# Batch statistics of a graph network: squares and two weight columns in place of a matrix product

## The chip, the cores and the metric

The kernel runs on 1 core of one Trainium2 chip. The time is the device time of one execution in microseconds (us). A core has five engines that run side by side and wait for each other by semaphores: TensorE (PE, with its weight loads as PEld), VectorE (DVE), ScalarE (ACT), GpSimd (POOL) and SyncE (SP).

## The reference

A node table x of 100,000 rows of 128 float32 goes through four residual blocks over one list of 50,000 edges sorted by destination: three GCN convolutions with batch normalization, two EVE convolutions, two SAGE convolutions, one GAT convolution. The change touches the first block alone:

```
for i in range(3):
    h = gcn_conv(h, src, dst, edge_weight, Ws[i], bs[i])
    h = h + x0
    if i < 2: h = relu(h)
    mean = mean(h, axis=0);  var = mean(square(h - mean), axis=0)
    h = (h - mean) * rsqrt(var + 1e-5) * gammas[i] + betas[i]
```

Mean and variance are taken over all 100,000 rows, so they are known only when a convolution has run through; the next one applies them as a scale and a shift of each feature.

## The kernel before

Rows of the node table are worked on in chunks of 1024 (128 partitions x T = 8 tiles of D = 128 features); two chunks are a node pair. There are 98 chunks, 49 pairs. Edges come in chunks of 1024, too, 49 of them, two to a step of the edge part.

`gcn_conv` (L1846) is called three times (stages m0, m1, m2). Each stage is one block in which every engine runs its own program, written by `merged_sweep` (L902): a loop over the edge pairs, and after each edge pair a loop over the node pairs that are ready, here mostly two. `run_conv` (L1812) gives the engines their parts.

GpSimd (`pool_program`, L1051) gathers source rows by indirect DMA (L1070, eight for a chunk of edges) and scatters edge results into a table of sums (L1078, eight for a chunk). It waits for the edge results that VectorE has read out (`e_out_read`, L1075). It gathers and scatters in steps of two chunks.

The edge part (`GcnEdges`, L1275): TensorE turns the gathered rows (L1119), ScalarE scales them in m1 and m2 (L1357), VectorE weighs them (L1366) and sums the runs of one destination (L1387), TensorE multiplies by the weights (L1129), VectorE scales the result (L1399).

The node part (`GcnNodes`, L1586) for node pair m:

- TensorE turns the pair's four half chunks (`turn_nodes`, L1187), multiplies the first two by the weights (`multiply_nodes`, L1205), then runs `between`, which is `add_gram` (L1621) for the pair before, and then multiplies the other two.
- ScalarE copies the turned halves to SBUF (L1222; L1220 in m0), then makes `y1` of the pair before from `acc` by a relu or a copy (L1652), then issues the two stores of `y1` (`store_before`, L1235, with the DMA at L1250).
- VectorE adds the residual to the sums (L1669), and makes `acc` of this pair from the multiplied halves, four instructions for each half (L1683).

The statistics before: `y1` has 129 columns, the last one all ones. For each of the eight tiles of a chunk TensorE multiplies the tile by itself (L1626), a 128x129 result that adds up in one PSUM bank `gram` over all chunks: its diagonal holds the sums of squares, its last column the sums. `vector_end` (L1696) multiplies the bank by the identity (L1703), reduces it (L1706) and works out scale and shift. The semaphore `finished` tells that `y1` is made; `gram_done` tells ScalarE that `y1` may be overwritten.

## Time and profile before

| | |
|---|---|
| median of 3 runs | 15559.0 us (15490.08 to 15566.16) |
| the profiled execution | 15524.1 us |
| its span in the profile | 15522.3 us |
| TensorE matmul busy | 7445.1 us, 48% |
| GpSimd busy | 7158.8 us, 46% |
| VectorE busy | 6201.3 us, 40% |
| ScalarE busy | 4643.8 us, 30% |
| matmuls of L1626 | 4800 records, 900.2 us busy |

Busy shares are averages over stages that differ. A row of a timeline gives the start in us, the time that it covers, the engine and line, the operation with out<-in, how many there are (x), and in brackets the idle time of the engine just before and what ended it. "issue" is time in which the engine waited for nothing that the profile shows; "remote" is a releaser that the profile doesn't name.

### The profile page before, as it was taken

What the parts mean: (1) busy time and instruction counts of PE and PEld (TensorE: products, weight loads), DVE (VectorE), ACT (ScalarE), POOL (GpSimd) and SP (SyncE); (2) the same over time, 40 slices, a digit from 0 to 9 for tenths busy, and PEclk for the clock granted to TensorE, in tenths of its full rate; (3) what the DMA queues carried; (4) which work ended last, traced back from release to release, by engine and by line L of the source; (5) the groups of instructions that cost most, each with busy time, mean ns of one, the idle gap of its engine ahead of it and who ended that gap; (6) DMA issues with size and microseconds to landing.
All of it is one profiled execution on the core that took longest, in us unless ns stands there. A gap on an engine that the chain in (4) does not pass through costs nothing. (4 is left out here: it accounts for less than half of the span.)

```text
span 15522.3 us, 166135 instructions
## 1 busy us (share of the span) xinstructions
PE 7445.1 (48%) x37142; PEld 5563.3 (36%) x37143; DVE 6201.3 (40%) x16108; ACT 4643.8 (30%) x8631; POOL 7158.8 (46%) x7582
## 2 busy tenths in 40 slices
PE   1024444544544448855555555533334445455554
PEld 1024444444434444333343333333333334233332
DVE  3333443334433435422223333322223333377778
ACT  1111111211111114422233333322213334266666
POOL 4644444444444440144434443345554444566663
PEclk9986776777767779877777777766667667677776
DMA  6965554666656667644454444445545555133333
GB/s 166 208 152 168 172 166 148 209 201 196 195 179 199 198 198 254 219 149 149 154 171 147 160 160 157 158 159 172 171 153 190 184 172 198 55 109 108 110 106 102
DMA packets 1864963, 2570.85 MB, mean 166 GB/s; under 512 B 255773, under 2 KB 1369141, under 8 KB 1864662
## 3 DMA queue, kind: packets, MB, share of 16 engines
q1 hardware_dynamic: 1134168, 1627.27, 32.8%
q10 hardware_dynamic: 504726, 564.87, 11.1%
q0 software_dynamic: 225792, 375.94, 8.4%
q14 instruction: 216, 1.77, 0.0%
q8 instruction: 61, 1.00, 0.0%
HBM read 1499.62 MB, written 1129.98 MB: 169 GB/s over the span
## 5 line engine op out<-in xcount | busy, mean ns | idle before, releaser
L1078 POOL DMA_INDIRECT sums_gcn<-m_result,m_idx x1176 | 1162.3, 988 | 2312.8 <-DVE m_result L1399 1953.1
L1220 ACT ACTIVATE m_nodeT<-m_n_bank 128x512 f32<-128x512 f32 x980 | 543.7, 597 | 4158.0 <-remote 2296.5
L1626 PE MATMUL m_gram<-m_y 128*128 128x129 f32 (+1 forms) x4800 | 900.2, 336 | 1752.2 <-issue 1440.3
L1683 DVE SCALAR_TENSOR_TENSOR m_acc<-m_n_bank,m_scales,m_res_b 128x128 f32<-128x128 f32 (+1 forms) x2352 | 645.4, 343 | 2566.0 <-remote 1863.1
L1078 POOL DMA_INDIRECT sums_eve<-m_result,m_idx x784 | 762.4, 972 | 1695.4 <-DVE m_result L1515 1470.5
L1187 PE MATMUL m_n_bank<-k_ident,m_in_y 128*128 128x128 f32 x5488 | 907.3, 323 | 1273.7 <-DVE m_z L1772 729.3
L1772 DVE TENSOR_TENSOR m_z<-m_n_bank,m_in_sums 128x512 f32<-128x512 f32 (+1 forms) x784 | 513.5, 687 | 2364.8 <-remote 1280.1
L1626 PEld LDWEIGHTS m_gram<-m_y 128*128 128x128 f32 (+1 forms) x4800 | 803.0, 246 | 1822.4 <-issue 1490.1
L1078 POOL DMA_INDIRECT sums_sage<-m_result,m_idx x784 | 762.4, 973 | 1378.3 <-DVE m_result L1399 1136.4
L1070 POOL DMA_INDIRECT m_rows<-node_rows_a,m_idx x1176 | 1124.5, 956 | 354.2 <-issue 338.0
L1187 PEld LDWEIGHTS m_n_bank<-k_ident,m_in_y 128*128 128x128 f32 x5488 | 763.3, 169 | 1402.6 <-DVE m_z L1772 808.4
L1222 ACT ACTIVATE m_nodeT<-m_n_bank,k_bn 128x512 f32<-128x512 f32 x392 | 285.4, 774 | 1939.1 <-PE m_n_bank L1187 1405.0
L1070 POOL DMA_INDIRECT m_rows<-node_rows_b,m_idx x784 | 749.7, 956 | 244.9 <-issue 233.6
L1205 PE MATMUL m_n_bank<-k_gcn,m_nodeT 128*128 128x128 f32 (+1 forms) x4704 | 701.9, 308 | 117.7 <-issue 89.3
L2215 POOL DMA_INDIRECT sums_gat<-g_result,g_idx x392 | 433.1, 1105 | 684.8 <-DVE g_result L2510 573.3
L1201 PE MATMUL m_n_bank<-m_in_x,k_ident 128*128 128x512 f32 (+1 forms) x784 | 473.3, 689 | 523.4 <-ACT m_nodeT L1220 344.9
L1119 PE MATMUL m_e_turn<-k_ident,m_rows 128*128 128x128 f32 x2744 | 495.9, 312 | 469.5 <-DVE m_sums L1582 219.0
L1205 PEld LDWEIGHTS m_n_bank<-k_gcn,m_nodeT 128*128 128x128 f32 (+1 forms) x4704 | 664.7, 223 | 151.4 <-issue 120.7
L1205 PE MATMUL m_n_bank<-k_self,m_nodeT 128*128 128x128 f32 x3136 | 470.0, 309 | 431.7 <-ACT m_nodeT L1220 392.4
L1205 PEld LDWEIGHTS m_n_bank<-k_self,m_nodeT 128*128 128x128 f32 x3136 | 462.4, 224 | 556.9 <-ACT m_nodeT L1220 401.7
L759 ACT ACTIVATE m_o<-m_z,m_ln_shift,m_ln_scale 128x128 f32<-128x128 f32 x1600 | 626.6, 479 | 90.3 <-DVE m_ln_shift L748 48.5
L1129 PE MATMUL m_e_out<-k_gcn,m_sums 128*128 128x128 f32 x2352 | 397.9, 322 | 512.8 <-DVE m_result L1399 400.5
(304 smaller groups left out, 17622.8 us busy)
## 6 DMA issues: line engine op xcount, KB each, us to landing
m_in_sums<-sums_gcn SPq DMA_DIRECT2D x291, 512.0 KB
m_in_y<-node_rows_a SPq DMA_DIRECT2D x291, 512.0 KB
sums_gcn<-k_gcn_b SPq DMA_DIRECT2D x194, 512.0 KB
node_rows_a<-m_y ACTq DMA_DIRECT2D x194, 512.0 KB
m_in_x<-in_x_dram SPq DMA_DIRECT2D x194, 512.0 KB
m_in_y<-node_rows_b SPq DMA_DIRECT2D x194, 512.0 KB
sums_eve<-k_eve_b SPq DMA_DIRECT2D x194, 512.0 KB
m_in_sums<-sums_eve SPq DMA_DIRECT2D x194, 512.0 KB
```

The source lines that it names most:

```text
L759: ins = act.activation(out[0:n, j, :], z[0:n, j, :], ACT.Identity, bias=self.shift[copy][0:n, at:at + 1], scale=self.scale[copy][0:n, at:a ...
L1070: pool.indirect_dma_start(self.rows[b][:, t, :], None, self.table[:, :], bass.IndirectOffsetOnAxis(self.idx[s][:, t:t + 1], 0)).then_inc(s ...
L1078: pool.indirect_dma_start(self.node_sums[:, :], bass.IndirectOffsetOnAxis(self.idx[s][:, T + t:T + t + 1], 0), self.result[b][:, t, :], No ...
L1119: mm = pe.transpose(bank[:, n * P:(n + 1) * P], self.rows[b][:, H * (i % 2) + n, 0:D], self.k["ident"][:, :])
L1187: mm = pe.transpose(self.n_bank[i][:, t * P:t * P + n], self.buf["y"][i // 2][0:n, H * (i % 2) + t, :], self.k["ident"][0:n, 0:n])
L1201: mm = pe.matmul(self.n_bank[i][0:n, :], self.k["ident"][0:n, 0:n], half.rearrange("p t f -> p (t f)"), start=True, stop=False)
L1205: mm = pe.matmul(self.n_bank[i][0:n, t * D:(t + 1) * D], self.nodeT[:, i, t * P:t * P + n], weight[:, :], start=not add, stop=not add or t ...
L1220: act.activation(out, src, ACT.Copy).then_inc(self.n_turn_read, 1)
L1626: mm = pe.matmul(self.gram[:, 0:D + 1], self.y1[b][0:rows[b], t, 0:D], self.y1[b][0:rows[b], t, :], start=False, stop=False, skip_group_ch ...
L1683: ins = dve.scalar_tensor_tensor(out=self.acc[b][0:n, tt, :], in0=ph.node_out(i, n)[:, t, :], scalar=self.scales[b][0:n, tt:tt + 1], in1=s ...
L1772: dve.tensor_tensor(self.z[b][0:n, half, :], ph.node_out(i, n), ph.buf["sums"][b][0:n, half, :], ALU.add).then_inc(ph.n_out_read, 1)
L2215: pool.indirect_dma_start(self.node_sums[:, :], bass.IndirectOffsetOnAxis(self.idx[s][:, T + t:T + t + 1], 0), self.result[b][:, t, :], No ...
```

## The change

`y1` loses its column of ones. ScalarE gets a second step for each chunk: after the stores of a pair are issued, it squares `y1` into a new buffer `ysq`. `add_gram` waits for the new semaphore `squared` in place of `finished`, and uses `picks`, two weight matrices of two columns (one column ones, the other zeros): the first puts the sum over the partitions of each column of `y1` into row 0 of the bank, the second that of `ysq` into row 1. The moving operand is half a chunk, 512 columns. `vector_end` copies the two rows, adds their four blocks of 128 to one, and has TensorE transpose the 2x128 result; the steps after that are the same with their counts moved by one.

```diff
--- before.py
+++ after.py
@@ -1598,20 +1598,23 @@
         self.res_b = [ph.sb(f"res_b{b}", [P, T, D]) for b in range(2)]
         self.acc = [ph.sb(f"acc{b}", [P, T, D]) for b in range(2)]
 
-        self.y1 = [ph.sb(f"y1{b}", [P, T, D + 1]) for b in range(2)]
+        self.y1, self.ysq = ([ph.sb(f"{n}{b}", [P, T, D]) for b in range(2)] for n in ("y1", "ysq"))
+        self.picks = ph.sb("picks", [P, 2, 2])
+        self.in_rows, self.pair_rows, self.col_rows = (ph.sb(n, [2, w]) for n, w in (("in_rows", 512), ("pair_rows", 256), ("col_rows", D)))
         self.scales = [ph.sb(f"scales{b}", [P, T]) for b in range(2)]
         self.small = ph.sb("small", [P, 8])
-        self.diag = ph.sb("diag", [P, D])
         self.gram = ph.ps("gram", [P, 512])
-        self.ones_set = ph.sem("ones_set")
+        self.ones_set, self.squared = ph.sem("ones_set"), ph.sem("squared")
         self.scales_set, self.added, self.acc_done = ph.sem("scales_set"), ph.sem("added"), ph.sem("acc_done")
         self.gram_done, self.bn_step, self.root_step = ph.sem("gram_done"), ph.sem("bn_step"), ph.sem("root_step")
         self.grants = [(ph.nodes_turned, 2)] + [(ph.used[n], 2) for n in ph.used] + [(s, 16) for s in ph.stored]
 
     def tensor_start(self, pe):
-        pe.wait_ge(self.ones_set, 2)
+        pe.wait_ge(self.ones_set, 3)
         zeros = self.ph.k["zeros"]
-        pe.matmul(self.gram[:, 0:D + 1], zeros[:, 0:P], zeros[:, 0:D + 1], start=True, stop=False, skip_group_check=True).then_inc(self.gram_done, 1)
+        for t in range(H):
+            mm = pe.matmul(self.gram[0:2, t * D:(t + 1) * D], zeros[:, 0:2], zeros[:, 0:D], start=True, stop=False, skip_group_check=True)
+        mm.then_inc(self.gram_done, 1)
 
     def tensor(self, pe, m, scattered):
         ph = self.ph
@@ -1621,17 +1624,21 @@
     def add_gram(self, pe, m, rows):
 
         for b in range(2):
-            pe.wait_ge(self.ph.finished, 2 * m + b + 1)
-            for t in range(T):
-                mm = pe.matmul(self.gram[:, 0:D + 1], self.y1[b][0:rows[b], t, 0:D], self.y1[b][0:rows[b], t, :], start=False,
-                               stop=False, skip_group_check=True)
+            pe.wait_ge(self.squared, 2 * m + b + 1)
+            for i, y in enumerate((self.y1[b], self.ysq[b])):
+                for h in range(2):
+                    mm = pe.matmul(self.gram[0:2, :], self.picks[0:rows[b], i, :],
+                                   y[0:rows[b], h * H:(h + 1) * H, :].rearrange("p t f -> p (t f)"), start=False, stop=False,
+                                   skip_group_check=True)
             mm.then_inc(self.gram_done, 1)
 
     def tensor_end(self, pe):
         last = self.ph.sh.node_chunks - 2
         self.add_gram(pe, self.ph.sh.node_pairs, (self.ph.sh.rows(last), self.ph.sh.rows(last + 1)))
+        pe.wait_ge(self.bn_step, 3)
+        pe.transpose(self.ph.n_bank[1][:, 0:2], self.col_rows[:, :], self.ph.k["ident"][0:2, 0:2]).then_inc(self.gram_done, 1)
         if self.last:
-            pe.wait_ge(self.bn_step, 12)
+            pe.wait_ge(self.bn_step, 13)
             for i in range(2):
 
                 pe.matmul(self.ph.n_bank[0][:, i * D:(i + 1) * D], self.as_rows[2][:, i, :], self.ph.k["ident"][:, :], start=True,
@@ -1649,8 +1656,12 @@
             act.wait_ge(self.acc_done, 2 * m + b + 1)
             ph.out_free(act, m, b)
             act.wait_ge(self.gram_done, 2 * m + 1)
-            act.activation(self.y1[b][0:n, :, 0:D], self.acc[b][0:n, :, :], ACT.Copy if self.last else ACT.Relu).then_inc(ph.finished, 1)
+            act.activation(self.y1[b][0:n, :, :], self.acc[b][0:n, :, :], ACT.Copy if self.last else ACT.Relu).then_inc(ph.finished, 1)
         ph.store_before(act, m, self.y1)
+        for b in range(2):
+            n = ph.sh.rows((m - 1) * 2 + b)
+            act.wait_ge(ph.finished, 2 * m + b + 1)
+            act.activation(self.ysq[b][0:n, :, :], self.y1[b][0:n, :, :], ACT.Square).then_inc(self.squared, 1)
 
     def finish_vector(self, dve, m):
         pass
@@ -1691,7 +1702,10 @@
     def vector_start(self, dve):
         for b in range(2):
             dve.memset(self.acc[b][:, :, :], 0.0).then_inc(self.acc_done, 1)
-            dve.memset(self.y1[b][:, :, D:D + 1], 1.0).then_inc(self.ones_set, 1)
+        dve.memset(self.picks[:, :, :], 0.0).then_inc(self.ones_set, 1)
+        dve.wait_ge(self.ones_set, 1)
+        for i in range(2):
+            dve.memset(self.picks[:, i, i:i + 1], 1.0).then_inc(self.ones_set, 1)
 
     def vector_end(self, dve):
 
@@ -1700,32 +1714,37 @@
         mean, sq, var, m2, root = (self.small[:, i:i + 1] for i in range(5))
         ss, step, gram = self.next_ss, self.bn_step, self.gram
         dve.wait_ge(self.gram_done, sh.node_chunks + 3)
-        dve.tensor_tensor(self.diag[:, :], gram[:, 0:D], k["ident"][:, :], ALU.mult).then_inc(step, 1)
-        dve.tensor_scalar(mean, gram[:, D:D + 1], 1.0 / sh.n, None, ALU.mult).then_inc(step, 1)
+        dve.tensor_copy(self.in_rows[:, :], gram[0:2, :]).then_inc(step, 1)
+        dve.wait_ge(step, 1)
+        dve.tensor_tensor(self.pair_rows[:, :], self.in_rows[:, 0:256], self.in_rows[:, 256:512], ALU.add).then_inc(step, 1)
         dve.wait_ge(step, 2)
-        dve.tensor_reduce(sq, self.diag[:, :], AX.X, ALU.add).then_inc(step, 1)
+        dve.tensor_tensor(self.col_rows[:, :], self.pair_rows[:, 0:D], self.pair_rows[:, D:2 * D], ALU.add).then_inc(step, 1)
+        sums = ph.n_bank[1]
+        dve.wait_ge(self.gram_done, sh.node_chunks + 4)
+        dve.tensor_scalar(mean, sums[:, 0:1], 1.0 / sh.n, None, ALU.mult).then_inc(step, 1)
+        dve.wait_ge(step, 4)
         dve.tensor_tensor(m2, mean, mean, ALU.mult).then_inc(step, 1)
-        dve.wait_ge(step, 4)
-        dve.scalar_tensor_tensor(out=var, in0=sq, scalar=1.0 / sh.n, in1=m2, op0=ALU.mult, op1=ALU.subtract).then_inc(step, 1)
         dve.wait_ge(step, 5)
+        dve.scalar_tensor_tensor(out=var, in0=sums[:, 1:2], scalar=1.0 / sh.n, in1=m2, op0=ALU.mult, op1=ALU.subtract).then_inc(step, 1)
+        dve.wait_ge(step, 6)
         dve.tensor_scalar(var, var, 0.0, BN_EPS, ALU.max, ALU.add).then_inc(step, 1)
-        dve.wait_ge(step, 6)
+        dve.wait_ge(step, 7)
         rsqrt(dve, root, var, sq, self.root_step, 0)
         dve.tensor_tensor(ss[:, 0:1], root, gamma[:, :], ALU.mult).then_inc(step, 1)
-        dve.wait_ge(step, 7)
+        dve.wait_ge(step, 8)
         dve.tensor_tensor(m2, mean, ss[:, 0:1], ALU.mult).then_inc(step, 1)
-        dve.wait_ge(step, 8)
+        dve.wait_ge(step, 9)
         dve.tensor_tensor(ss[:, 1:2], beta[:, :], m2, ALU.subtract).then_inc(step, 1)
-        dve.wait_ge(step, 9)
+        dve.wait_ge(step, 10)
         if self.last:
             for i in range(2):
                 dve.tensor_scalar(self.as_rows[2][:, i, :], k["ones"][:, :], ss[:, i:i + 1], None, ALU.mult).then_inc(step, 1)
-            dve.wait_ge(step, 11)
+            dve.wait_ge(step, 12)
             dve.sem_inc(step, 1)
-            dve.wait_ge(self.gram_done, sh.node_chunks + 5)
+            dve.wait_ge(self.gram_done, sh.node_chunks + 6)
             for i in range(2):
                 dve.tensor_copy(self.as_rows[i][:, :], ph.n_bank[0][:, i * D:(i + 1) * D]).then_inc(step, 1)
-            dve.wait_ge(step, 14)
+            dve.wait_ge(step, 15)
 
 
 class LinearNodes:
```

## Rows read from the trace of the kernel before

**Rows 1.** The page: the span.

```profile
span 15522.3 us, 166135 instructions
```

**Rows 2.** Line L1626 by itself: durations in ns (least, median, most), first and last start.

```profile
L1626 PE MATMUL m_gram<-m_y x4800: 270/276/584, 1031.1 to 5929.1; 128*128 128x129 f32 x192
```

**Rows 3.** Waits in m1, 2562 to 4250: us in total, times, longest.

```profile
POOL sums_gcn L1078 <- DVE m_result L1399: 661.5, 25, 42.7
DVE m_acc L1683 <- remote: 623.8, 40, 30.9
...
PE m_gram L1626 <- issue: 503.0, 228, 12.5
```

**Rows 4.** Timeline of POOL in m1: two bursts' ends, and a longer pause.

```profile
2842.12 1.01 POOL L1078 DMA_INDIRECT sums_gcn<-m_result,m_idx  x1 [42.68 <-DVE m_result L1399]
...
3047.11 1.01 POOL L1078 DMA_INDIRECT sums_gcn<-m_result,m_idx  x1 [27.59 <-DVE m_result L1399]
...
3087.62 0.95 POOL L1070 DMA_INDIRECT m_rows<-node_rows_a,m_idx  x1 [0.30 <-issue]
3115.94 1.01 POOL L1078 DMA_INDIRECT sums_gcn<-m_result,m_idx  x1 [27.37 <-DVE m_result L1399]
```

**Rows 5.** Timeline of TensorE in the same cycle.

```profile
3053.14 1.95 PE L1205 MATMUL m_n_bank<-k_gcn,m_nodeT 128*128 128x128 f32 x16
3061.80 4.24 PE L1626 MATMUL m_gram<-m_y 128*128 128x129 f32 x18 [6.72 <-issue]
3067.08 0.38 PE L1626 MATMUL m_gram<-m_y 128*128 128x129 f32 x1 [1.04 <-issue]
...
3093.38 3.62 PE L1205 MATMUL m_n_bank<-k_gcn,m_nodeT 128*128 128x128 f32 x16
3096.80 2.32 PE L1187 MATMUL m_n_bank<-k_ident,m_in_y 128*128 128x128 f32 x16
...
3101.63 3.84 PE L1626 MATMUL m_gram<-m_y 128*128 128x129 f32 x32 [0.72 <-ACT m_y L1652]
3105.30 1.95 PE L1205 MATMUL m_n_bank<-k_gcn,m_nodeT 128*128 128x128 f32 x16
```

**Rows 6.** Timeline of ScalarE, the same cycle and the next (3138.40).

```profile
3063.15 3.89 ACTq L1250 DMA_DIRECT2D node_rows_b<-m_y  x2
...
3100.51 2.02 ACT L1652 ACTIVATE m_y<-m_acc 128x1024 f32<-128x1024 f32 x2
3102.99 1.40 ACTq L1250 DMA_DIRECT2D node_rows_b<-m_y  x2
...
3138.40 6.57 ACTq L1250 DMA_DIRECT2D node_rows_b<-m_y  x2
```

**Rows 7.** Timeline of VectorE, the same cycle.

```profile
3093.02 1.13 DVE L1683 SCALAR_TENSOR_TENSOR m_acc<-m_n_bank,m_scales,m_res_b 128x128 f32<-128x128 f32 x4 [15.35 <-remote]
...
3106.75 2.16 DVE L1683 SCALAR_TENSOR_TENSOR m_acc<-m_n_bank,m_scales,m_res_b 128x128 f32<-128x128 f32 x8 [2.53 <-PE m_n_bank L1205]
```

**Rows 8.** Stretches: length, busy of PE, PEld, DVE, ACT, POOL, clock, DMA share, GB/s.

```profile
3057.00:3060.00 3.00, 0.00 (x0) 0.00 (x0) 0.00 (x0) 0.12 (x1) 2.28 (x3) 1.00 0.13 50
3060.00:3063.00 3.00, 1.20 (x5) 1.20 (x6) 0.00 (x0) 2.67 (x3) 2.39 (x3) 0.51 0.53 143
```

**Rows 9.** Timeline of TensorE in the second EVE convolution: 512-column matmuls.

```profile
9036.08 2.07 PE L1201 MATMUL m_n_bank<-m_in_x,k_ident 128*128 128x512 f32 x2 [19.61 <-ACT m_nodeT L1220]
...
9041.69 1.02 PE L1201 MATMUL m_n_bank<-m_in_x,k_ident 128*128 128x512 f32 x2
9042.55 1.05 PE L1205 MATMUL m_n_bank<-k_self,m_nodeT 128*128 128x128 f32 x8
```

**Rows 10.** Waits in the first SAGE convolution, 10034 to 11510.

```profile
POOL sums_sage L1078 <- DVE m_result L1399: 472.3, 26, 40.6
```

**Rows 11.** Timeline of VectorE at the end of m1.

```profile
4245.84 0.29 DVE L1703 TENSOR_TENSOR m_diag<-m_gram,k_ident 128x128 f32<-128x128 f32 x1 [4.87 <-PE m_gram L1626]
...
4249.51 0.16 DVE L1718 TENSOR_TENSOR k_bn<-k_beta,m_small 128x1 f32<-128x1 f32 x1
```

## The prediction

> **What bounds the kernel now.** I read the page first. No engine is busy for half of the span [rows 1], so this is a kernel of waits, and the page's chain of waits speaks only of the last convolution. The changed lines run in three stages, m0, m1 and m2 (the GCN convolutions). The history of the product line is the next view: 4800 matmul records of 270/276/584 ns [rows 2], 1600 for each stage. A float32 matmul stands as two records, and one node pair has 16 matmuls, so 32 records are one pass of the statistics and a stage has 50 passes. I take m1 (2562 to 4250 us) for all three.
>
> Then the waits inside m1 [rows 3]. GpSimd waited 25 times and 661.5 us for VectorE's edge results, a mean of 26.5 us. The statistics matmuls idled 503.0 us "until issue", which is no wait for a producer that the profile knows. VectorE's accumulation waited 623.8 us for something remote.
>
> The timelines tell why. GpSimd works in bursts: indirect transfers from 3047.11 to 3088.57, then a pause of 27.37 us, next burst at 3115.94 [rows 4]. Burst plus pause is 68.8 us, and some 24 of them fill the stage. The burst's length is GpSimd's own, so whatever lengthens or shortens the pause moves the stage. One cycle holds two node pairs. The first pair's pass runs during the burst and crawls: 18 records go at once from 3061.80, after them single ones more than 1 us apart (3067.08 is one), and the other half of the multiplication comes only at 3093.38, some 5 us after the last transfer [rows 5]. That is 31.6 us for a pass whose twin in the pause takes 3.67 us (3101.63 to 3105.30) [rows 5]. VectorE shows the same crawl from its side: an accumulation whose matmul had ended by 3055.1 starts at 3093.02 [rows 5, 7]. So in a burst the pass is cheap to lengthen, up to a point, and in the pause it is paid in full. The pause in which a third node pair falls is 42.68 us instead of 27.37 [rows 4]: an exposed pair costs 15.3 us and nothing hides it.
>
> The count follows. A crawling pass idles about 31.6 - 3.84 = 27.8 us here; 503.0 us of such idling make some 18 to 20 crawling passes in a stage. I take 20 crawling and 30 exposed, and of those 30 drop one, the first, which lies in the short first burst. 29 exposed, 20 crawling, per stage.
>
> **The change part by part.**
>
> *Exposed pass, start.* Before, the pass starts when the first of the two y1 activations ends. Now it needs a square, and ScalarE squares only after both y1 (3100.51 + 2.02 = 3102.53) and after the issue of both stores (3102.99 + 1.40 = 3104.39) [rows 6]. A square reads and writes the same 128x1024 values as a y1 activation, two of which took 2.02 us; I take 1.05 us, and 0.3 us for the waits and the end of the branch ahead of it. The first square is done at about 3105.8 to 3105.9, against a start at 3101.63: +4.25 us. The second is done 1 us later and is never late. Nothing else can fill this time: TensorE's second half of the multiplication stands behind the pass, VectorE's last two accumulations wait for it (2.53 us of waiting already at 3106.75 [rows 7]), and the edge part, GpSimd's results with it, stands behind VectorE.
>
> *Exposed pass, length.* 32 records of 129 columns go, 16 records of 512 columns come (eight matmuls, two records each). That is 8192 columns in place of 4128. A pair of 512-column records took 0.86 us from its start to that of the next operation (9041.69 to 9042.55) [rows 9], so 16 take 6.9 us; the old pass took 3.67 us. +3.2 us. The 128-column weight loads that vanish were hidden: 32 loads and 32 matmuls together took 0.115 us each [rows 5]. The Trainium skill (page "TensorE: Matmul & The Clock Gate", section "LDWEIGHTS (loading the stationary operand)") prices a load by its columns, about 107 ns for 128; if that stood in the open, 32 loads would be 3.4 us, the length would come out even and the sum near 15,880 us. The row above shows that it doesn't stand in the open, and the estimate isn't used.
>
> *Exposed pass, clock.* TensorE now idles from 3100.9 to 3105.9 ahead of it. After an idle start at 3055.09 the granted clock was 1.00 until 3060 and 0.51 in the next 3 us [rows 5, 8], which are the levels 2.4 and 1.2 GHz. A pair of 512-column records took 2.07 us at the lower level against 1.02 [rows 9]. The clock comes back within a few us of steady work: 16 records took 3.62 us, the next 16 took 2.32, the next 1.95 [rows 5]. I take +1.2 us; bounds 0 (clock stays) and 6.9 (low all through). Together an exposed pass costs +8.6 us, bounds +7.4 and +14.3.
>
> *Crawling pass.* TensorE puts through 32 matmuls and loads fewer, so at the end of the crawl it has the second half of the multiplication behind it, too, which before took 3.62 us from 3093.38. But VectorE's second accumulation can't start ahead of 3093.02, where TensorE's older signal arrived; three accumulations of 1.13 us follow, and end at about 3096.5 where they ended at 3098.17. Against it stand two squares and their waits on ScalarE, behind store issues that end at 3067.04 in one burst and at 3144.97 (11.6 us ahead of the burst's end) in the next [rows 6]; with some 5 us for the squares and 7 to 14 us for the matmuls the pass still ends near where it did. I take -2 us per pass; bounds -4 (the clock is up as well) and +3 (the late burst spills over).
>
> *Waits added.* ScalarE's next work behind the squares is the next pair's turned rows or the edge activation, and both wait for TensorE operations that stand behind the pass itself, so the squares' 2.1 us cost nothing more there. SyncE and GpSimd run the same instructions; the loads that VectorE's signal frees move with it.
>
> *Ends.* At the end of each stage the diagonal product and its reduction (two of 0.29 us in the chain that starts at 4245.84 and ends 3.8 us later [rows 11]) give way to one 2x512 copy, two small adds and a transpose on TensorE with a wait each way: +1.3 us a stage, bounds 0 and 4. The new starting memsets and four small zero matmuls in place of one lie at the start beside the first gathers: 0, at most 2.
>
> *Sum.* Per stage 29 x 8.6 - 20 x 2 + 1.3 = 211 us, for three stages 633 us. The profiled execution took 15524.1 us (span 15522.3), which gives 16,157; I say 16,160 us. That run lies 0.2% below the shown median of 15559.0 and inside its runs of 15490 to 15566. With the bounds that are likely together: 29 x 7.45 - 20 x 4, three times, gives 15,930; 29 x 12 + 0, three times, gives 16,570.
>
> **Rivals.**
>
> *A, the crawl is relieved further (still slower).* If the crawl is a limit on how many instructions get through, halving the pass's instructions could free the other engines too. The sage stage has two node pairs a cycle as well and no statistics, and GpSimd's pauses there are 472.3 us over 26 [rows 10], mean 18.2 us. Add a whole new exposed pass (8.6 + 4.4 of the old one with its wait, 13.0) and the pause is 31.2, 4.7 us above 26.5: 25 x 4.7 x 3 gives about 15,880. Against it: the old signal at 3093.02 doesn't depend on what is queued behind it.
>
> *B, faster.* One mechanism: in the burst the first pair is through so early that the second pair's pass gets into the burst as well. It decides at 29 x 8.6 / 20 = 12.5 us won per crawling pass; the pause would be the sage stage's 18.2, 8.3 us less than now, 25 x 8.3 x 3 = 620 us off: 14,900. For it: 503 us of crawling sit on exactly the instructions that are halved. Against it: the second pair needs VectorE's accumulations, which the crawl holds back and the change doesn't touch. The Trainium skill (page "Runtime: NRT & Kernel Launch", section "Instruction fetch mechanics") says that a jump out of the loaded window forces a fetch; were that the crawl, a shorter loop body would end it in this way. The second pass in the same loop doesn't crawl, and the crawl ends with the burst [rows 4, 5], so I give it no more than that chance. At the deciding point itself the time would be about 15,520 (no change).
>
> *C, the squares get stuck.* ScalarE crawls in the burst as well (two store issues took 6.57 us there, 1.40 in the pause [rows 6]). If the squares are seen only when the crawl ends, the matmuls follow in the open: +9 us per crawling pass, (29 x 8.6 + 20 x 9) x 3 = 1290: 16,810.
>
> **How the numbers follow.** Forecast 0.58, A 0.15, C 0.15, B 0.07, no change (relief at the deciding point) 0.05. What a measurement of this kernel can tell from no change is about 0.5%, 78 us. Faster by more: 0.07; within: 0.05; slower: 0.88. The range holds A and the forecast and nearly reaches C's value: 15,850 to 16,770.
>
> **What would show it.** In the pause, the first statistics record starts about 4.3 us later behind the y1 pair, 16 records take 7 to 9 us, and the granted clock dips ahead of them; GpSimd's pause grows from 27.4 to 33 to 35 us while the burst stays at 41 us; stages m0 to m2 grow by about 210 us each and no other stage moves. In the burst, the second half of the multiplication is done by about 3093 in the cycle's own terms. I am wrong if the pause stays at 27 us or less, if the pass starts before the store issues end, or if 512-column records of the pass don't take 0.43 us each at full clock.

## The result, and the profile after

| | before | after |
|---|---|---|
| median | 15527.15 us (5 runs, 15490.08 to 15566.16) | 16061.56 us (5 runs, 15986.65 to 16087.5) |
| profiled execution | 15524.1 us | 15992.39 us |
| ratio | | 1.0327 (95% interval 1.0303 to 1.0351) |
| m0, m1, m2, profiled (from the first clearing of `acc` to the next, m2 to the reading of the bank) | 1666, 1690, 1678 us | 1839, 1857, 1847 us |
| GpSimd's waits for edge results in m0 to m2 | 1953.1 us | 2432.7 us |

The change costs 3.3%. The ratio is worked out from all runs of the pair; the two medians alone lie 534 us apart. The profiled executions lie 468 us apart, and in them GpSimd's waits in the three changed stages grew by 479.6 us. Its waits of the same kind in the EVE, SAGE and GAT stages moved by +23, +0.5 and -55 us. Each changed stage grew by 167 to 173 us, 509 us in all, and the rest of the kernel took 41 us less. That rest is the same code in every kernel of this text. Behind m2 it took 9518 to 9682 us in the eleven profiles of the table below, whatever was done to the statistics, so a good part of the scatter between runs lies there, and the three stages show an edit more sharply than the total does.

The page of the kernel after: the span, and the DMA queue of ScalarE's stores (packets, MB, share).

```profile
span 15990.5 us, 161683 instructions
...
q10 hardware_dynamic: 242226, 564.87, 10.0%
```

The same megabytes had stood as 504726 packets at 11.1%. y1's rows are 128 wide now, so a partition's eight tiles lie in one piece. The prediction had not seen this.

The waits in m1 of the kernel after, 2730 to 4587 us (us in total, times, longest), against [rows 3]:

```profile
POOL sums_gcn L1078 <- DVE m_result L1399: 816.8, 25, 50.7
...
DVE m_acc L1694 <- remote: 557.8, 37, 33.3
...
PE m_gram L1630 <- issue: 214.9, 17, 19.7
...
PE m_gram L1630 <- ACT m_ysq L1664: 163.6, 33, 11.9
```

The same 25 waits, 155 us longer. The statistics idle for less "until issue", and for the first time they wait for ScalarE.

GpSimd's timeline, first transfers of three bursts, against [rows 4]. The full bursts keep their length (41.06 us on the mean in both kernels), the pauses of 27.4 us are now 31 to 34:

```profile
3031.82 1.00 POOL L1078 DMA_INDIRECT sums_gcn<-m_result,m_idx  x1 [50.71 <-DVE m_result L1399]
...
3104.28 1.01 POOL L1078 DMA_INDIRECT sums_gcn<-m_result,m_idx  x1 [31.90 <-DVE m_result L1399]
...
3179.23 1.01 POOL L1078 DMA_INDIRECT sums_gcn<-m_result,m_idx  x1 [33.49 <-DVE m_result L1399]
```

TensorE in those cycles, against [rows 5]. The burst ends at 3072.39:

```profile
3059.85 3.58 PE L1630 MATMUL m_gram<-m_y,m_picks 128*2 128x512 f32 x4 [17.72 <-issue]
...
3069.38 1.05 PE L1205 MATMUL m_n_bank<-k_gcn,m_nodeT 128*128 128x128 f32 x7
3071.94 0.27 PE L1205 MATMUL m_n_bank<-k_gcn,m_nodeT 128*128 128x128 f32 x1 [1.51 <-issue]
3075.44 0.37 PE L1205 MATMUL m_n_bank<-k_gcn,m_nodeT 128*128 128x128 f32 x1 [3.23 <-issue]
3076.85 1.67 PE L1205 MATMUL m_n_bank<-k_gcn,m_nodeT 128*128 128x128 f32 x7 [1.05 <-issue]
...
3087.52 1.88 PE L1630 MATMUL m_gram<-m_y,m_picks 128*2 128x512 f32 x4 [3.63 <-ACT m_ysq L1664]
...
3092.67 1.88 PE L1630 MATMUL m_gram<-m_ysq,m_picks 128*2 128x512 f32 x4
3094.48 2.05 PE L1205 MATMUL m_n_bank<-k_gcn,m_nodeT 128*128 128x128 f32 x16
...
3159.72 2.70 PE L1630 MATMUL m_gram<-m_y,m_picks 128*2 128x512 f32 x4 [3.75 <-ACT m_ysq L1664]
3162.21 2.80 PE L1630 MATMUL m_gram<-m_ysq,m_picks 128*2 128x512 f32 x4
```

Within the burst the 16 statistics records now go through in one piece (to 3069.4) and the crawl falls on the multiplication behind them. In the pause a pass waits for the square. It then takes 6.96 us (3087.52 to 3094.48), or 8.65 us when its first half runs at a lower clock, as from 3159.72. ScalarE and VectorE in the first of these pauses, against [rows 6, 7]:

```profile
3082.78 1.99 ACT L1659 ACTIVATE m_y<-m_acc 128x1024 f32<-128x1024 f32 x2
3085.23 0.99 ACTq L1250 DMA_DIRECT2D node_rows_b<-m_y  x2
3086.41 2.00 ACT L1664 ACTIVATE m_ysq<-m_y 128x1024 f32<-128x1024 f32 x2 [1.64 <-issue]
```

```profile
3070.21 1.13 DVE L1694 SCALAR_TENSOR_TENSOR m_acc<-m_n_bank,m_scales,m_res_b 128x128 f32<-128x128 f32 x4 [29.40 <-remote]
3076.95 1.12 DVE L1694 SCALAR_TENSOR_TENSOR m_acc<-m_n_bank,m_scales,m_res_b 128x128 f32<-128x128 f32 x4 [5.61 <-remote]
...
3096.03 2.16 DVE L1694 SCALAR_TENSOR_TENSOR m_acc<-m_n_bank,m_scales,m_res_b 128x128 f32<-128x128 f32 x8 [9.12 <-PE m_n_bank L1205]
```

The squares come behind both y1 and both store issues, so the pass starts 4.74 us behind the start of the first y1 (3087.52 against 3082.78), where the old pass started 1.12 us behind it. VectorE then waits 9.12 us for the multiplication behind the pass; before it waited 2.53. The accumulation at 3070.21 also shows that what was held up in a burst need not wait for its end: it starts 2.2 us ahead of the end of the burst at 3072.39, where the one at 3093.02 in the kernel before started 4.4 us behind its burst [rows 4, 7].

The granted clock (the number behind the five engines' busy times) in the first 3 us of the two passes:

```profile
3087.60:3090.60 3.00, 3.00 (x8) 0.59 (x9) 0.00 (x0) 0.82 (x1) 0.00 (x0) 1.00 1.01 401
3159.80:3162.80 3.00, 3.00 (x5) 0.43 (x5) 0.00 (x0) 0.81 (x1) 0.00 (x0) 0.64 1.01 408
```

**One cycle in four parts.** Each kernel has 54 cycles in m0 to m2 with a full burst (over 40 us) and behind it a pause that holds the pass of one node pair. The short bursts at both ends of a stage, and pauses with two passes, are not among them. A pause splits into: from the burst's last transfer to the first y1 (what the crawl left behind), from there to the pass, the pass, and from the pass to the next burst. The means are worked out from the timelines, in us. "m0 to m2" is the length of the three stages in the one profiled execution. The last column is the time, as the ratio to the kernel before on the same chip times 15,527.

| kernel | burst end to y1 | y1 to pass | pass | pass to burst | pause | m0 to m2 | time |
|---|---|---|---|---|---|---|---|
| before | 11.92 | 1.12 | 3.84 | 10.05 | 26.92 | 5,034 | 15,527 |
| after | 9.59 | 4.74 | 8.04 | 10.25 | 32.62 | 5,543 | 16,035 |
| e1, the wait alone | 11.62 | 5.20 | 6.27 | 10.22 | 33.32 | 5,516 | 16,010 |
| e2, the length alone | 9.73 | 1.36 | 7.03 | 10.14 | 28.26 | 5,153 | 15,662 |
| e3, 256 columns | 11.72 | 4.76 | 8.72 | 10.16 | 35.36 | 5,709 | 16,204 |
| e4, rows of 129 | 9.76 | 5.16 | 8.61 | 10.26 | 33.78 | 5,623 | 16,126 |
| e5, before with rows of 128 | 11.73 | 1.11 | 3.84 | 10.08 | 26.76 | 5,010 | 15,526 |
| e6, rows, then squares | 9.71 | 1.30 | 7.17 | 10.12 | 28.29 | 5,162 | 15,678 |
| e10, squares first | 9.64 | 2.99 | 7.03 | 10.25 | 29.91 | 5,318 | 15,830 |
| e7, old pass last | 11.35 | 2.32 | 3.74 | 6.56 | 23.97 | 4,843 | 15,294 |
| e12, new pass last | 10.40 | 2.76 | 7.03 | 6.67 | 26.86 | 5,039 | 15,563 |

### The profile page after: what moved, and what is told of

The parts are those of the page before. It is cut to its first block and busy times, and to the rows that moved or that the text cites. A ratio compares the mean times of both kernels' runs of the same rounds, so it can differ in the third digit from the quotient of the medians.

```text
span 15990.5 us, 161683 instructions
## 1 busy us (share of the span) xinstructions
PE 7924.2 (50%) x34763; PEld 4994.7 (31%) x34764; DVE 6196.5 (39%) x16114; ACT 4955.6 (31%) x8931; POOL 7173.9 (45%) x7582
## 5 line engine op out<-in xcount | busy, mean ns | idle before, releaser
L1078 POOL DMA_INDIRECT sums_gcn<-m_result,m_idx x1176 | 1164.1, 990 | 2792.4 <-DVE m_result L1399 2432.7
L1187 PE MATMUL m_n_bank<-k_ident,m_in_y 128*128 128x128 f32 x5488 | 986.8, 342 | 1353.9 <-DVE m_z L1791 831.0
L1187 PEld LDWEIGHTS m_n_bank<-k_ident,m_in_y 128*128 128x128 f32 x5488 | 811.2, 177 | 1539.1 <-DVE m_z L1791 908.2
L1630 PE MATMUL m_gram<-m_y,m_picks 128*2 128x512 f32 (+1 forms) x1200 | 733.7, 745 | 1111.1 <-issue 652.6
L1630 PE MATMUL m_gram<-m_ysq,m_picks 128*2 128x512 f32 (+1 forms) x1200 | 645.4, 665 | 0.0
```

The lines of the kernel that those rows point to most:

```text
L1078: pool.indirect_dma_start(self.node_sums[:, :], bass.IndirectOffsetOnAxis(self.idx[s][:, T + t:T + t + 1], 0), self.result[b][:, t, :], No ...
L1187: mm = pe.transpose(self.n_bank[i][:, t * P:t * P + n], self.buf["y"][i // 2][0:n, H * (i % 2) + t, :], self.k["ident"][0:n, 0:n])
L1630: mm = pe.matmul(self.gram[0:2, :], self.picks[0:rows[b], i, :], y[0:rows[b], h * H:(h + 1) * H, :].rearrange("p t f -> p (t f)"), start=F ...
```

## The experiments

**e1: the wait without the new matmuls.** The edit to the kernel before:

```diff
-            pe.wait_ge(self.ph.finished, 2 * m + b + 1)
+            pe.wait_ge(self.squared, 2 * m + b + 1)
...
+            act.activation(self.ysq[b][0:n, :, :], self.y1[b][0:n, :, 0:D], ACT.Square).then_inc(self.squared, 1)
```

> The kernel before with one part of the change: ScalarE also squares the rows behind both stores, and the product pass waits for the squares, which nothing reads. Theory (start of the pass costs): an exposed pass starts 3.6 us later behind y1 (4.74 in the kernel after, 1.11 in the kernel before), its length stays 3.84 or grows to about 4.7 where the clock falls first; 87 exposed passes at 3.6 to 4.5 us are 315 to 390 us, so 15,840 to 15,920. Rival (the wait runs beside another wait and only the length costs): within 60 us of the kernel before.

Measured: 16,021 us, ratio 1.0311 (1.0270 to 1.0352). That is 101 us above the expected band, on the side of the theory; the rival is out. The start was as expected for rows of 129 (5.20 us behind y1). The clock cost more: nearly the whole short pass ran at the lower level, not only its first records. One pass of e1, and the first 3 us of it:

```profile
3527.46 6.33 PE L1627 MATMUL m_gram<-m_y 128*128 128x129 f32 x32 [4.66 <-ACT m_ysq L1658]
```

```profile
3527.50:3530.50 3.00, 3.00 (x14) 3.00 (x15) 0.00 (x0) 0.86 (x1) 0.00 (x0) 0.50 1.01 333
```

The granted clock is 0.50 in these 3 us, the level of 1.2 GHz, and 0.64 in the next 3. In the 54 cycles the pass took 5.2 to 6.8 us, never the 3.84 of before. So the wait alone, with the same matmuls as before, costs nearly what the whole change costs.

**e2: the new matmuls without the wait.** The edit to the kernel after; ScalarE's squares are gone too:

```diff
-            pe.wait_ge(self.squared, 2 * m + b + 1)
-            for i, y in enumerate((self.y1[b], self.ysq[b])):
+            pe.wait_ge(self.ph.finished, 2 * m + b + 1)
+            for i, y in enumerate((self.y1[b], self.y1[b])):
```

> The kernel after without the squares: the pass waits for y1 as before and reads y1 twice with the two weight columns (the sums of squares are left out). Theory: the pass starts 1.1 us behind y1a, stays at the full clock and lasts 7.0 us, so 87 exposed passes cost 3.2 us each (+278), the 60 passes in a burst give back 3 us each (-180): 15,600 to 15,660. Rival (start and length both lie on the path, and the burst gives nothing back): 15,800. Rival (the 7 us lie beside VectorE's work): 15,350 to 15,450.

Measured: 15,675 us, ratio 1.0087 (1.0057 to 1.0118). That is 15 us above the expected band, with the interval reaching into it, and both rivals are out. The pass took 7.03 us in 53 of the 54 cycles, +3.19, and the pause began with 2.2 us less of crawl. With 0.3 us at the start of the pass and behind it a full cycle is 1.34 us longer. Over 54 cycles that is 72 us of the 119 by which m0 to m2 grew; the rest lies in the first and last cycles of the stages.

**e3 and e4: where the shorter crawl comes from.** e3 brings the 32 records back, with no other change to the columns; e4 brings the rows of 129 back, and everything that uses `y1` takes its first 128 columns:

```diff
-                for h in range(2):
-                    mm = pe.matmul(self.gram[0:2, :], self.picks[0:rows[b], i, :],
-                                   y[0:rows[b], h * H:(h + 1) * H, :].rearrange("p t f -> p (t f)"), start=False, stop=False,
+                for h in range(4):
+                    mm = pe.matmul(self.gram[0:2, h % 2 * 256:h % 2 * 256 + 256], self.picks[0:rows[b], i, :],
+                                   y[0:rows[b], h * 2:h * 2 + 2, :].rearrange("p t f -> p (t f)"), start=False, stop=False,
```

```diff
-        self.y1, self.ysq = ([ph.sb(f"{n}{b}", [P, T, D]) for b in range(2)] for n in ("y1", "ysq"))
+        self.y1, self.ysq = ([ph.sb(f"{n}{b}", [P, T, w]) for b in range(2)] for n, w in (("y1", D + 1), ("ysq", D)))
...
```

> The kernel after with 256 columns a matmul: 32 records and 32 weight loads a pass as in the kernel before, with the same columns as in the kernel after. Theory (the burst gives back time because fewer records queue in it): the 3 us for each of 60 passes in a burst are lost again, +180 us on the kernel after (16,240), while an exposed pass stays at 7.0 to 8.7 us. Rival (what comes back in the burst is due to y1's rows of 128, whose stores have half the packets): no change from the kernel after, within 40 us of 16,060.

> The kernel after with y1's rows again 129 wide, so that its stores go out in packets of 512 bytes, 504,726 of them on ScalarE's queue instead of 242,226. Theory (records in the burst): only the two store issues grow from 0.99 to 1.40 us ahead of the squares, 0.4 us for 87 passes, +35 us on the kernel after (16,095). Rival (the packets give the time back): +120 to +180 us (16,180 to 16,240).

Measured: e3 16,187 us, ratio 1.0436 (1.0393 to 1.0478), 125 us above the kernel after instead of the 180 expected, and outside its rival's band. e4 16,128 us, ratio 1.0386 (1.0347 to 1.0425), 33 us above the figure expected and 52 below its rival's band, so neither as stated. The four parts tell them apart. With 32 records the burst end to y1 is 11.72 us again, as in the kernel before; with rows of 129 it stays at 9.76. TensorE in a burst of e3:

```profile
3337.47 1.67 PE L1630 MATMUL m_gram<-m_y,m_picks 128*2 128x256 f32 x7
3339.58 0.38 PE L1630 MATMUL m_gram<-m_y,m_picks 128*2 128x256 f32 x1 [0.43 <-issue]
...
3359.18 0.59 PE L1630 MATMUL m_gram<-m_ysq,m_picks 128*2 128x256 f32 x1 [2.21 <-issue]
3361.28 0.37 PE L1205 MATMUL m_n_bank<-k_gcn,m_nodeT 128*128 128x128 f32 x1 [1.52 <-issue]
3361.99 3.56 PE L1205 MATMUL m_n_bank<-k_gcn,m_nodeT 128*128 128x128 f32 x15 [0.34 <-issue]
```

The last records of the pass drip again, that is, they go one by one with up to 2.4 us between them, and the multiplication runs after them. How far TensorE gets can be counted in the bursts' timelines. From the start of the pass in a burst to the first idle time over 0.4 us went (records of the multiplication behind it included) 17 to 21 records in most bursts of the kernel before (129 columns, median 19, in 4.3 us), 21 to 25 in e3 (256 columns, median 23, in 6.9 us) and 22 to 25 in the kernel after (512 columns, median 24, in 10.3 us). The time differs by a factor of 2.4 between the first and the last and the columns by 4, the count by a quarter; and e1, with the matmuls of the kernel before, has 20 to 24. What is given back in the burst comes from the number of records. It is 2.1 to 2.3 us a cycle. The rest of e3's longer pause is its pass, 8.72 against 8.04 us: 5 of its 54 passes took 7.1 us, the length at full clock, where 23 of the kernel after took 7.0.

e4 costs 0.42 us more at the start (its two store issues are 1.40 us long) and 0.57 us more of lowered clock in the pass: +1.16 us a pause, 63 us over 54 cycles, of the 80 us that m0 to m2 are longer. In e4 46 of the 54 passes took 8.7 us, in the kernel after 29: the later start is what the expectation priced, the clock behind it is what it left out. So rows of 128 do help the new kernel, by a shorter issue that stands ahead of the squares.

**e5: rows of 128 in the kernel before.** The column of ones, and with it the means, is left out.

> The kernel before with y1 in rows of 128, without the column of ones (the sums of y1, so the means, are left out): its stores go out in packets of 4,096 bytes, nothing else changes. Theory: in the kernel before the pass does not stand behind the store issues, so the 0.4 us of shorter issue and the smaller number of packets bring 0 to 30 us: 15,500 to 15,540. Rival (the packets hold up what runs in a burst): 15,400 or less.

Measured: 15,518 us, ratio 0.9999 (0.9975 to 1.0023). That is inside the expected band; the rival is out. Half as many packets on the queue bring nothing where no one waits for the issue.

**e6: rows first, then squares.** The edit to the kernel after (the matmuls below it then read `y[b]`, and `gram_done` is counted up in the second round alone):

```diff
-        for b in range(2):
-            pe.wait_ge(self.squared, 2 * m + b + 1)
-            for i, y in enumerate((self.y1[b], self.ysq[b])):
+        for i, (ready, y) in enumerate(((self.ph.finished, self.y1), (self.squared, self.ysq))):
+            for b in range(2):
+                pe.wait_ge(ready, 2 * m + b + 1)
```

> The whole statistics of the kernel after in another order: TensorE first sums the rows of both halves, on y1 alone, then the squares of both. Theory: the first 8 records (3.5 us) fill the time in which ScalarE issues the stores and squares, so the pass starts 1.1 us behind y1a, the clock stays at 1.00, and it ends about 8.3 us behind y1a, as in the run without squares: 15,660 to 15,720. Rival (ScalarE's squares themselves hold up the node work behind them): 15,800 or more.

Measured: 15,688 us, ratio 1.0097 (1.0061 to 1.0133), as expected and as e2, where no squares are made. Half of the pass now fills the wait for the squares:

```profile
3990.84 3.60 PE L1630 MATMUL m_gram<-m_y,m_picks 128*2 128x512 f32 x8
3994.48 3.59 PE L1630 MATMUL m_gram<-m_ysq,m_picks 128*2 128x512 f32 x8
```

The same statistics in another order take back 2.3 of the 3.3%.

**e10: the squares ahead of the stores.** In `finish_scalar` the loop with the squares is put before `store_before`.

> The kernel after with the squares ahead of both store issues. Theory: the pass starts 3.7 us behind y1a instead of 4.74, TensorE idles 2.6 us ahead of it, so that the clock stays at 1.00 and the pass at 7.03 us in every cycle (mean 8.2 in the kernel after): 2.2 us for 87 passes, 190 us less than the kernel after, 15,850 to 15,900. Rival (the stores, 2 us later, hold up the next y1 or the burst): 15,980 to 16,060.

Measured: 15,853 us, ratio 1.0195 (1.0154 to 1.0237), as expected in size. The start was better than I had it (2.99 us behind the first y1, not 3.7) and the clock stayed up, as expected: 7.03 us for the pass in each of the 54. The later stores cost nothing that shows: the parts ahead of y1 and behind the pass are 9.64 and 10.25 us, against 9.59 and 10.25.

```profile
3999.38 1.88 PE L1630 MATMUL m_gram<-m_y,m_picks 128*2 128x512 f32 x4 [2.01 <-ACT m_ysq L1663]
```

**e7: the old pass behind the last multiplication.** The edit to the kernel before, in `multiply_nodes`:

```diff
         for i in range(4):
-            if i == 2 and between:
-                between()
...
             mm.then_inc(self.n_multiplied, 1)
+        if between:
+            between()
```

> The kernel before with the product pass behind the last multiplication of a node pair instead of between the second and the third. Theory (the exposed pass costs because VectorE's additions of the third and fourth multiplication wait for it): these start 3.8 us earlier in 87 exposed cycles, while the pass runs beside them: 15,200 to 15,350. Rival (the edge matmuls behind the node work then wait for the same pass): within 50 us of the kernel before.

Measured: 15,302 us, ratio 0.9850 (0.9814 to 0.9886): inside the expected band, faster than both kernels and the fastest on this kind of chip. TensorE and VectorE in one pause of e7:

```profile
3078.37 3.74 PE L1203 MATMUL m_n_bank<-k_gcn,m_nodeT 128*128 128x128 f32 x32
3081.95 3.74 PE L1626 MATMUL m_gram<-m_y 128*128 128x129 f32 x32
3085.52 0.60 PE L1119 MATMUL m_e_turn<-k_ident,m_rows 128*128 128x128 f32 x4
```

```profile
3081.10 2.16 DVE L1683 SCALAR_TENSOR_TENSOR m_acc<-m_n_bank,m_scales,m_res_b 128x128 f32<-128x128 f32 x8 [0.60 <-ACT m_y L1652]
3083.84 2.16 DVE L1683 SCALAR_TENSOR_TENSOR m_acc<-m_n_bank,m_scales,m_res_b 128x128 f32<-128x128 f32 x8 [0.58 <-DVE m_acc L1683]
```

All four multiplications are done before the pass, and VectorE's two accumulations (3081.10 to 3086.00) run beside it. The pass ends at 3085.5, when VectorE would not have been free anyway. Most of the 3.84 us is hidden: 2.95 us of pause are gone, 2.39 of them behind y1 and 0.57 ahead of it.

**e8, e9, e11: three kernels on a chip that runs them faster.** e8 is e6 with the pass last, e11 is the kernel after with the pass last, e9 is the kernel before with one product a half chunk in place of eight.

> Rows then squares (as in the run with rows first), and the pass behind the last multiplication of the pair. Theory: the third and fourth multiplication no longer wait for 8.3 us of pass; VectorE's additions cover about 4 us of it, as with the product pass, where 2.7 us an exposed pass came back: 235 to 350 us less than with rows first (15,690), so 15,340 to 15,460. Rival (the longer pass now holds up the edge matmuls behind it): no gain, 15,640 to 15,700.

> The kernel before with one product a half instead of eight, 4 records a pass instead of 32 (the statistics are left out but for one tile in eight). Theory: an exposed pass costs 3.4 us less (87 times, 295 us), and in a burst 28 fewer records at the 0.13 us a record that the run with 256 columns showed (125 us over 60 passes and 16 records) give 3.6 us in 60 passes (220 us): 15,000 to 15,080. Rival (records in the burst are free, only the exposed length counts): 15,230 to 15,260.

> The kernel after with nothing changed but the place of the pass: behind the last multiplication. Theory: VectorE's additions no longer wait for squares and pass (12 us behind y1a), but the edge matmuls behind it do; the pass ends as late as before less the 2 us of the multiplications that now fill the wait, so 87 exposed passes give back 4 to 5 us each: 15,620 to 15,720. Rival (the wait for squares goes on holding TensorE for as long, and the edges for as much): 15,950 to 16,060.

Measured, on one chip: the kernel before 10,917 us (19 runs, 10,893.59 to 10,929.37), e8 10,924 (ratio 1.0010, 1.0000 to 1.0019), e9 10,901 (0.9984, 0.9974 to 0.9993), e11 11,153 (1.0224, 1.0207 to 1.0241). The kernel before is the very program that takes 15,530 us elsewhere, so none of the three tests its expectation. They show something else. GpSimd's waits and the busy row (PE, PEld, DVE, ACT, POOL, clock, DMA share, GB/s) of e8 in 2000 to 2900 us, within m1:

```profile
POOL sums_gcn L1078 <- issue: 102.4, 336, 0.3
POOL m_rows L1070 <- issue: 101.0, 352, 0.3
```

```profile
2000.00:2900.00 900.00, 741.83 (x3862) 455.98 (x3863) 573.51 (x1685) 364.88 (x439) 693.67 (x742) 0.93 0.90 325
```

There is no pause: 760 transfers follow each other from 1964.4 to 2944.1, and TensorE's passes go through in one piece beside them (8 records in 3.60 us). Nothing crawls, and GpSimd's own issue sets the stage. The statistics cost next to nothing there, long or short: e9 without most of them gains 0.2%, e8 with the long ones loses 0.1%. Of the three only e11, where TensorE also stands still for the squares, makes GpSimd wait again. GpSimd's waits of e11 in the same stretch (the wait of this name is 0.3 us in e9 and does not appear in e8):

```profile
POOL sums_gcn L1078 <- DVE m_result L1399: 59.3, 17, 9.1
```

**e12: e8 once more, on a chip of the first kind.**

> The kernel of the run e8 again, for a chip on which the kernel before takes 15,540 us and TensorE's records drip in GpSimd's bursts. Theory there: VectorE's additions cover about 4 us of the 7.2 us pass, as with the product pass, where 2.7 us an exposed pass came back: 235 to 350 us less than with rows first (15,690), so 15,340 to 15,460. Rival (the longer pass then holds up the edge matmuls by all it no longer holds up the additions): 15,640 to 15,700. On a chip where the kernel before takes 10,920 us: 10,920 as in e8, within 30 us.

Measured: 15,497 us against 15,473, ratio 1.0023 (1.0009 to 1.0036). It misses the band by 37 us, and by about 100 on the scale of the table, since this chip ran the kernel before in 15,473 us and not in 15,540. It gains 0.7% on e6, some 115 us, where I expected 235 to 350. The rival is out as well, so neither held as stated. In m0 to m2 it takes 5039 us, the kernel before 5034. TensorE and VectorE in a pause:

```profile
3976.17 3.74 PE L1203 MATMUL m_n_bank<-k_gcn,m_nodeT 128*128 128x128 f32 x32
...
3983.27 3.60 PE L1630 MATMUL m_gram<-m_ysq,m_picks 128*2 128x512 f32 x8
3986.80 0.66 PE L1119 MATMUL m_e_turn<-k_ident,m_rows 128*128 128x128 f32 x4
```

```profile
3981.64 2.16 DVE L1695 SCALAR_TENSOR_TENSOR m_acc<-m_n_bank,m_scales,m_res_b 128x128 f32<-128x128 f32 x8 [0.58 <-DVE m_acc L1695]
...
3988.27 0.70 DVE L1366 TENSOR_TENSOR m_e_turn<-m_e_turn,m_w_all 128x512 f32<-128x512 f32 x1 [3.80 <-ACT m_e_turn L1357]
```

The accumulations end at 3983.8, the pass 3 us later, and VectorE stands still for 3.80 us ahead of the first edge chunk. The additions cover most of an old pass, and only part of a new one. In the burst, 16 more records lie ahead of the pass and it drips again (burst end to y1 10.40).

## Why the prediction was right

The time, 16,062 us, lies 0.6% below the 16,160 predicted. Of the 633 us forecast, 534 came, and 509 in the three stages of the profile. The mechanism is the predicted one: every term has the predicted sign, and the shortfall is a sum of small ones, not one error covered by another. By its own steps:

- **Exposed pass, start, +4.25 us.** Right in its parts. The kernel after has +3.62, since the two store issues shrank from 1.40 to 0.99 us with rows of 128, and the rest came 0.2 us sooner. e1 and e4 keep rows of 129 and have +4.08 and +4.04. This is the one thing that the diff held and I did not read: the lost column changes the stores as well.
- **Exposed pass, length, +3.2 us.** Right: 7.03 against 3.84, +3.19. Records of 512 columns took 0.43 us each, so the cost is the number of columns, twice as many as the product had; e3 streams as many in 32 records and takes 7.1 us where the clock is full.
- **Exposed pass, clock, +1.2 us.** Right in the mean, +1.01 (8.04 against 7.03), and it is a mean of two cases: 23 passes of 7.0 us and 31 of 8.7 to 9.7. The sign that was named, a clock that dips ahead of the records, did not show. The granted clock was 1.00 in the idle time ahead of both passes shown (3084 to 3087.5, 3156 to 3159.7), stayed at 1.00 in the first and fell in the second only when its records had begun (0.64). The 0.41 us saved at the issue also spares some of the passes the lower clock: in e4 the mean is 8.61.
- **Crawling pass, -2 us.** Right: -2.33 from the burst's end to y1. e3 shows that it is the number of records, e4 and e5 that it is not the packets. In the one cycle that the prediction followed, the second half of the multiplication was to be done by about 3093 in the old cycle's terms, 4.4 us behind the burst's last transfer. It ends 6.1 us behind it (3078.5), where before it ended 8.4 us behind: sooner by 2.3 us, but not by 4. The reason given for the bound, a signal to VectorE that arrives at 3093.02 whatever TensorE has queued, was read from one cycle. The last long wait (over 8 us) of VectorE's accumulations ends inside the burst in 25 of the 54 cycles before and in 24 after. The bound held on the mean: that wait ends 0.6 us behind the burst in both kernels.
- **Waits added, 0.** Right for what the squares themselves hold up: with the same 16 matmuls e6 (squares made) and e2 (none) have pauses of 28.29 and 28.26 us.
- **Ends, +1.3 us.** The chain from the bank to the shift takes 5.2 us (4578.11 to 4583.3, with the last step at 4583.14) where it took 3.8, +1.4:

```profile
4578.11 0.68 DVE L1717 COPY m_in_rows<-m_gram 2x512 f32<-2x512 f32 x1 [13.15 <-PE m_gram L1630]
...
4583.14 0.16 DVE L1737 TENSOR_TENSOR k_bn<-k_beta,m_small 128x1 f32<-128x1 f32 x1
```

- **Sum, 211 us a stage.** Too large by some 40: 167 to 173. The start term is 0.63 us smaller, times 29, 18 us; the clock term gives 5 and the crawl 7. The remaining 11 or so come from the ends of a stage. In m1, 19 cycles have one pass in the pause in both kernels and grew by 104 us in all. The first two and the last three have short bursts or two passes in one pause (the last three grew from 25, 23 and 25 us to 38, 38 and 34). These five grew by 63 us, where the 10 exposed passes that the sum has left for them would be 78 at the 7.8 us measured (3.62, 3.19 and 1.01); against these 15 stand some 4 us, since the way from the pass to the burst is 0.2 us longer in each of the 19. "No other stage moves" can't be judged to better than the scatter of the rest (GAT's waits fell by 55 us).
- **Rivals.** A named a time of 15,880 us by a mean pause of 31.2 us. The 25 pauses of m1 have a mean of 32.7 (816.8 us), between A's and the 34.9 that the forecast comes to (26.5 + 211/25), and a little nearer to A's. The number doesn't decide between them, the parts do: A needs other engines freed, and VectorE's long waits end where they did; the shortfall of the forecast lies in the start, the clock and the ends of the stages, and the crawl gave back 2.33 us, not much more than the 2 forecast. B did not come about: the passes in the burst got through sooner, but by 2.3 us and not by 12.5. The fetch of instructions that B was linked with finds no support: e12 crawls and e8, the same program, does not, and their instruction queues moved the same packets (171 and 58). C did not either: in all 54 cycles ScalarE's squares of the burst were done at least 8 us ahead of its end (3060.8 against 3072.4 in the cycle shown).

The two parts of the change, alone, cost 3.1% (e1) and 0.9% (e2), and together 3.3%. They don't add up. In the cycles of the table the short pass of e1 runs nearly all at the lower clock (+2.43 us), the long one only for its first part (+1.01), and e1 still has the issue of 1.40 us.

## What to carry to other kernels

Ask first what a new operand waits for, and only then what the new instruction costs: here the wait behind two stores, by itself, cost nearly as much as the whole change, and summing the part that was ready first took most of it back. A piece of work that nobody downstream needs soon belongs behind the piece that someone does: moving the old pass past two multiplications won 1.5%, more than any form of the pass. It hides only as much as the neighbour's work is long (of the old pass of 3.8 us most was hidden, of the new one of 7.0 only part).

## What the runs showed of the hardware

- **Chips that differ.** The kernel before took 15.43 to 15.59 ms on chips 11, 12 and 14 and 10.89 to 10.93 ms on chip 3, and the kernel of e8 and e12 10.92 and 15.50 ms. Which chip the first comparison ran on isn't known; its times are those of the three. In the profiles from the three TensorE's records drip while GpSimd issues indirect transfers, and VectorE's accumulations start late, some within the burst and some behind it (by 4.4 us at 3093.02 in the kernel before). In those from chip 3 nothing of this shows. GpSimd's own transfers don't tell the two apart: in e8 and e12, the same program, a scatter into the sums took 0.97 us in both. Nor does the traffic of the instruction queues, 171 and 58 packets in both. What makes the difference stays open; no run tests it, and as each chip was used for one set of runs only, it isn't shown that the chip itself is the cause. The change itself was not run on chip 3. The ratios of this text, with those named of e8, e9 and e11 excepted, hold for the three.
- **The crawl goes by records.** About 17 to 25 records of a pair go at once in a burst, and the rest drips, whether they have 129, 256 or 512 columns. So 16 records of 512 columns go in one piece in the kernel after, 32 of 256 do not (e3), and 512-column records drip too when 16 more records stand ahead of them (e12). What sets the count stays open.
- **A lowered clock cost the short pass more than the long one.** After 4.66 us of idle TensorE, 32 records of 129 columns took 6.33 us, the first 3 us of them at 0.50 of the clock, where they take 3.84. The 16 longer records took 8.65 us after 3.75 us of idle time, and 6.96 after 3.63.
